# Layer norm statistics in five groups, key constants of two groups set by GpSimd, and a store wait split in two

## The reference

```
q, k, v = y @ Wq.T + bq, y @ Wk.T + bk, y @ Wv.T + bv      # y = layernorm(x), 16 heads of 8
attn    = softmax(q k^T / sqrt(8)) * head_mask
x       = x + (attn v) @ Wo.T + bo
z       = layernorm(x)
x       = x + shared_ffn(z) + sum over the top 2 of 8 experts of gate_e * ffn_e(z)
```

## Time and profile before

| | |
|---|---|
| median of 3 runs | 617.31 us |
| the profiled execution | 620.32 us |
| its span | 618.5 us |
| PE busy | 601.8 us, 97% |
| DVE busy | 494.4 us, 80% |
| ACT busy | 445.3 us, 72% |
| POOL busy | 281.0 us, 45% |
| granted TensorE clock | 0.999 of full speed |

### The profile page before, as it was taken

One profiled execution on the slowest core, in us unless ns is written; L12 is line 12 of the kernel. 1 busy time (PEld: TensorE's weight loads), 2 busy tenths in 40 slices (PEclk: granted clock), 3 DMA queues, 4 the chain that ended last, 5 costly groups with the idle time before them and its releaser, 6 DMA issues. The chain is left out here.

```text
span 618.5 us, 21763 instructions
## 1 busy us (share of the span) xinstructions
PE 601.8 (97%) x8263; PEld 389.9 (63%) x8263; DVE 494.4 (80%) x1077; ACT 445.3 (72%) x967; POOL 281.0 (45%) x481
## 2 busy tenths in 40 slices
PE   7999999999999999999999999999999999999998
PEld 3544555555445545545545545447899999989966
DVE  8899999998988988988988988536366666666557
ACT  5878988888888888887887887973455555555551
POOL 7946711422641642542542542566454445545510
PEclk9999999999999999999999999999999999999999
DMA  6887343342443131131131230003222222212174
GB/s 174 246 279 210 86 98 89 111 113 79 122 123 88 55 95 47 54 97 51 50 96 50 51 97 12 17 31 78 53 66 65 64 68 60 68 56 66 47 263 153
DMA packets 43983, 57.66 MB, mean 93 GB/s; under 512 B 11146, under 2 KB 31754, under 8 KB 43898
## 3 DMA queue, kind: packets, MB, share of 16 engines
q1 hardware_dynamic: 39578, 47.59, 27.3%
q0 software_dynamic: 4320, 8.89, 4.4%
HBM read 35.76 MB, written 20.42 MB: 91 GB/s over the span
## 5 line engine op out<-in xcount | busy, mean ns | idle before, releaser
L1020 DVE TENSOR_REDUCE mx<-ps 128x2 f32<-128x1024 f32 x256 | 304.1, 1211 | 28.1 <-PE ps L1460 23.7
L883 ACT ACTIVATE probs<-ps 128x512 f32<-128x512 f32 x512 | 290.0, 601 | 46.4 <-PE ps L1488 32.7
L1488 PE MATMUL ps<-q_op,k_op 128*32 128x512 bf16 x2048 | 199.9, 380 | 2.2 <-ACT probs L883 1.2
L1460 PE MATMUL ps<-k_op,q_op 96*32 96x512 bf16 x2048 | 158.2, 380 | 2.6 <-DVE mx L1020 2.0
L1503 PE MATMUL ps<-probs,v_op 128*32 128x256 f32 x2048 | 157.6, 378 | 0.2 <-ACT probs L883 0.2
L941 ACT ACTIVATE probs<-ps,b_cur 128x128 f32<-128x128 f32 x284 | 80.9, 368 | 67.2 <-PE ps L1704 54.1
L759 POOL DMA_INDIRECT results<-rest,row_id x71 | 73.0, 1028 | 77.1 <-DVE rest L1330 60.0
L1488 PEld LDWEIGHTS ps<-q_op,k_op 128*32 128x32 bf16 x2048 | 58.6, 95 | 59.4 <-ACT probs L883 11.9
L650 POOL DMA_INDIRECT slots<-route_sb,slot_u x64 | 63.6, 993 | 68.8 <-ACT probs L883 59.5
L1460 PEld LDWEIGHTS ps<-k_op,q_op 96*32 96x32 bf16 x2048 | 55.1, 96 | 61.4 <-DVE mx L1020 22.1
L1503 PEld LDWEIGHTS ps<-probs,v_op 128*32 128x32 f32 x2048 | 65.3, 109 | 41.6 <-issue 0.9
(11 more groups left out here) (180 smaller groups left out, 554.2 us busy)
## 6 DMA issues: line engine op xcount, KB each, us to landing
q_op<-q_scr SPq DMA_DIRECT2D x96, 96.0 KB
k_op<-k_scr SPq DMA_DIRECT2D x96, 96.0 KB
w_sb<-in_W SPq DMA_DIRECT2D x18, 256.0 KB
probs<-slots SPq DMA_DIRECT2D x71, 64.5 KB
q_scr<-w_sb SPq DMA_DIRECT2D x8, 384.0 KB, 3.7
k_scr<-w_sb SPq DMA_DIRECT2D x8, 384.0 KB, 3.9
k_scr<-w_sb SPq DMA_DIRECT2D x8, 256.0 KB, 4.4
probs<-results SPq DMA_DIRECT2D x4, 512.0 KB, 4.8
```

The costliest lines, as they stand in the source:

```text
L883: nc.scalar.activation(probs[:, i, j, :], ps[:, BANK["key", b, hg, s], :], ACT.Exp, scale=float(D) ** -0.5).then_inc(s_exp, 1)
L1020: nc.vector.reduce_max(mx[:, slot % 2, 2 * p:2 * p + 2], ps[:, bank:bank + 2, :], AX.X).then_inc(s_max, 1)
L1460: last = nc.tensor.matmul(ps[c, BK_A + a % 4, :], q_op[hg][0:SH, j, P * i + c.start:P * i + c.stop], k_op[hg][0:SH, j, :], start=True, sto ...
L1488: last = nc.tensor.matmul(ps[c, bank, :], k_op[hg][:, j, P * i + c.start:P * i + c.stop], q_op[hg][:, j, :], start=True, stop=True)
```

## The change

The statistics of sequences 4 to 7 become two groups: {4, 5}, made where the group of four was, and {6, 7}, made by VectorE in sequence 2, with their power and product on GpSimd after the third parts of sequence 2. The minus ones of head groups 2 and 3 are set by GpSimd, over all 128 rows of `k_op`, and the zeros are written over rows 0 to 95 afterwards; for group 3 all of this moves from sequence 1 to sequence 3. The stores of sequence 0 get semaphores of their own, one for q and one for k, and the first group's loads are issued q first, three of q after the q store has landed, then three of k after the two k stores have. `wait_stored` gives all other users of the store semaphores the same waits as before, with the counts of `s_scr[0]` lower by one round. Blank lines are left out:

```diff
         s_w1st, s_wom = sem("first_weights_loaded"), sem("wo_masked")
+        s_q0, s_k0 = sem("first_q_parts_stored"), sem("first_k_parts_stored")
...
+        def wait_stored(eng, b):
+
+            if b == 0:
+                eng.wait_ge(s_q0, 16)
+                eng.wait_ge(s_k0, 16 * (N_SCR - 1))
+            elif b > 0:
+                eng.wait_ge(s_scr[b % DEEP], (b // DEEP + (b % DEEP > 0)) * (16 * N_SCR))
+
...
-        LN1_SEQS = ((0,), (1,), (2, 3), (4, 5, 6, 7))
+        LN1_SEQS = ((0,), (1,), (2, 3), (4, 5), (6, 7))
         POOL_SEQ = 3
         LN1_TILES = [slice(NT * some[0], NT * (some[-1] + 1)) for some in LN1_SEQS]
         LN1_OF = [n for n, some in enumerate(LN1_SEQS) for _ in some]
...
                 sp.wait_ge(s_lo, 2 * b + 1)
-                sp.dma_start(to_q, parts[u][:, 0, :, :]).then_inc(s_scr[u], 16)
+                sp.dma_start(to_q, parts[u][:, 0, :, :]).then_inc(s_scr[u] if b else s_q0, 16)
                 sp.wait_ge(s_mid, 2 * b + 2)
                 sp.wait_ge(s_lo, 2 * b + 2)
-                sp.dma_start(to_k[:, 0:PARTS, :], parts[u][:, 1, :, :]).then_inc(s_scr[u], 16)
-                sp.dma_start(to_k[:, PARTS:K_PARTS, :], parts[u][:, 1, 0:K_PARTS - PARTS, :]).then_inc(s_scr[u], 16)
+                sp.dma_start(to_k[:, 0:PARTS, :], parts[u][:, 1, :, :]).then_inc(s_scr[u] if b else s_k0, 16)
+                sp.dma_start(to_k[:, PARTS:K_PARTS, :], parts[u][:, 1, 0:K_PARTS - PARTS, :]).then_inc(s_scr[u] if b else s_k0, 16)
             def load_group(b, hg):
                 wait(sp, s_sb, (b * HG + hg - HG + 1) * (J * NT))
                 if b == 0:
                     sp.wait_ge(s_zero[hg], N_ZERO)
-                if hg == 0:
-                    sp.wait_ge(s_scr[b % DEEP], (b // DEEP + 1) * (16 * N_SCR))
-                for r in range(PARTS):
-                    for scr, op, first in ((q_scr, q_op, 0), (k_scr, k_op, D * r)):
-                        src = scr[b, :, :].rearrange("(x h) t -> x h t", h=H)[first:first + PR, J * hg:J * (hg + 1), :]
-                        sp.dma_start(op[hg][PR * r:PR * (r + 1), :, :], src).then_inc(s_ld[hg], 16)
+                if hg == 0 and b > 0:
+                    wait_stored(sp, b)
+                uses = [(r, w) for r in range(PARTS) for w in range(2)]
+                if (b, hg) == (0, 0):
+                    uses.sort(key=lambda use: use[1])
+                for r, w in uses:
+                    if (b, hg, r) == (0, 0, 0):
+                        sp.wait_ge((s_q0, s_k0)[w], 16 * (1, N_SCR - 1)[w])
+                    scr, op, first = ((q_scr, q_op, 0), (k_scr, k_op, D * r))[w]
+                    src = scr[b, :, :].rearrange("(x h) t -> x h t", h=H)[first:first + PR, J * hg:J * (hg + 1), :]
+                    sp.dma_start(op[hg][PR * r:PR * (r + 1), :, :], src).then_inc(s_ld[hg], 16)
...
                 if e == 0:
                     for u in range(DEEP):
-                        sp.wait_ge(s_scr[u], (B // DEEP) * (16 * N_SCR))
+                        wait_stored(sp, B - DEEP + u)
...
             def zero_scores(hg):
                 nc.gpsimd.memset(q_op[hg][:, :, :].bitcast(f32), 0.0).then_inc(s_zero[hg], 1)
+                if hg >= 2:
+                    nc.gpsimd.memset(k_op[hg][:, :, :].bitcast(f32), TWO_MINUS_ONES).then_inc(s_zero[hg], 1)
+                    pool.wait_ge(s_zero[hg], 2)
                 nc.gpsimd.memset(k_op[hg][0:SH, :, :].bitcast(f32), 0.0).then_inc(s_zero[hg], 1)
...
                 if b == 0:
                     normalise(POOL_SEQ)
                     ln1_rstd(3)
-                elif b == 1:
+                elif b == 3:
                     zero_scores(3)
                 elif b == 2:
+                    ln1_rstd(4)
                     nc.gpsimd.memset(v_op[:, :, :, :, :], 0.0).then_inc(s_pad, 1)
                     pool.wait_ge(s_pad, 2)
                     for hg in range(HG):
...
                 ready, bias, bank = ((s_qp, bq_sb, q_bank(b)), (s_kp, bk_sb, k_bank(b)))[w]
                 act.wait_ge(ready, b + 1)
-                wait(act, s_scr[b % DEEP], b // DEEP * (16 * N_SCR))
+                wait_stored(act, b - DEEP)
                 nc.scalar.activation(parts[b % DEEP][:, w, 0, :], ps[:, bank, :], ACT.Identity, bias=bias[:, 0:1]).then_inc(s_hi, 1)
...
             def ln1_stats(n):
                 some = LN1_TILES[n]
-                dve.wait_ge(s_x[n], 16)
+                dve.wait_ge(s_x[min(n, 3)], 16)
                 for t in range(some.start, some.stop):
                     last = nc.vector.bn_stats(stats[:, t, :], x_sb[:, t, :])
                 last.then_inc(s_st, 1)
...
                 if b == 0:
                     ln1_stats(3)
                     ln1_moments(3)
-                if b in (1, 2):
-                    set_key_ones(1 + b)
+                if b == 2:
+                    ln1_stats(4)
+                    ln1_moments(4)
                 first_max(b, 2)
```

## The result

The changed kernel is slower: median 619.39 us (616.75 to 621.18, 20 runs) against 617.63 us (616.6 to 619.02, 20 runs), a ratio of 1.0024 with a 95% interval of 1.0015 to 1.0033. I had forecast 616.1 us, from the 617.31 us of the first three runs. The single executions fall in two clusters. Six of the 20 have a mean granted clock of 0.999 or 1.0 and a median of 617.18 us; fourteen have 0.997 or 0.994 and a median of 619.91.

The account below looks back on a forecast made before the run. TensorE's long stretch bounds the kernel, its start set by ScalarE's chain in the projection stage. A gain of 1.22 us, other edits adding nothing, gave 617.31 - 1.22 = 616.1 us; range 615.3 to 617.7.

Parts of the forecast that it names:

- The path through the group of 16: Projection stage: eight tiles instead of 16 free VectorE 1.61 us earlier; ScalarE's k part of sequence 2 comes 1.22 earlier.
- The sets moved off VectorE: Two constant sets, 2.36 us with issue, leave VectorE for GpSimd; little worth alone, but make room for the moved tiles.
- the earlier loads: On SP, q loads go before k loads, the last issued 1.1 us earlier; worth 0 alone, protecting up to 1.1.
- the moved half: Eight tiles of statistics moved into sequence 2 on VectorE take 2.40 us; cost 0.0, at most 0.1, or 0.2 uncovered.
- The cover: VectorE's idle 1.01 us before 29.13, taken to cover its 0.2 us lag behind ScalarE at the remainder of sequence 3.
- Rival 3: GpSimd's constant sets, at about 30.5 to 33.4, hold VectorE by up to 2.85 us: 618.9 us; chance 0.08.
- Rival 1: The k loads land late, delaying row scores to 24.3; 0.3 to 0.6 gain left, 616.7 to 617.0 us; chance 0.12.
- Rival 2: The TensorE-bound stretch sets its own start, so earlier inputs only wait and nothing is gained: 617.3 us; chance 0.12.
- the power of sequences 2 and 3: On GpSimd, behind the added constant set, its issue was forecast 0.15 us later; cost 0, at most 0.1.

Follow-up runs that it names:

- r2: Changed kernel with GpSimd taking the fifth group's power before the third parts in sequence 2; 598.52 us, ratio 0.9985 to the kernel before.
- r8: The kernel before the change, unchanged, profiled again on another chip; 600.09 us in one run.
- r6: Kernel of r2 with the minus ones of head groups 2 and 3 set by VectorE again; 602.26 us, ratio 1.0045 to the kernel before.
- r5: Kernel of r2 without the split store wait, loads of the first group as before the change; 598.73 us, ratio 0.9989 to the kernel before.
- r4: Changed kernel with statistics in four groups again, keeping GpSimd's constants and the split wait; 599.41 us, ratio 0.9999 to the kernel before.
- r9: Changed kernel with GpSimd's third parts of sequence 2 replaced by constant sets that read nothing; 619.41 us, ratio 0.9980 to the kernel before.
- r1: The changed kernel as it is, run again on another chip; 601.09 us, ratio 1.0024 to the kernel before.
- r3: Changed kernel with six more unused matmuls on TensorE after the row scores of sequence 3; 599.52 us, ratio 1.0001 to the kernel before.
- r10: Kernel of r2 with none of the five keeping matmuls before the first transposes; 619.16 us, ratio 0.9973 to the kernel before.

## Why the prediction was wrong

**Right: where the gain comes from and how large it is.** The path through the group of 16, ScalarE's idle time and TensorE's k projection, 1.22 us with 0.39 of 1.61 lost, stands, though VectorE came 1.27 us earlier and not 1.61: it was TensorE's k projection that set ScalarE's k part, at 18.89 on the old scale as forecast. r2 shows the gain, 38.30 to 37.08 (and 38.35 in r8, its wait of 0.38 taken off). The whole kernel gained 0.9 of it. The sets moved off VectorE are what lets it through (r6), and the earlier loads spare TensorE an idle time of 1.51 (r5's profile); by themselves both are worth nothing (r4).

**The step that failed: the moved half.** "Cost of the moved half: 0.0, at most 0.1; if the cover were gone, 0.2." I took the length of the group, 2.40 us, from a place where GpSimd, beside the seven steps, only set constants or stood idle, and moved it beside the third parts of sequence 2. There it takes 4.01 us from the start of its tiles to the start of its last step (21.54 to 25.55), and r9 shows the cause: without the reads of the third parts the same three steps take 0.17 at most. The remainder of sequence 3 came 1.55 us later than forecast, not 0.0 to 0.2. I had checked for each engine when its operand would be there, and not what the two do to each other while both are busy. The cover that I had named, 1.01 us before 29.13, was on the wrong side: TensorE's q projection of sequence 4 asks for the remainder itself, since it writes over its bank, and does so 1.2 us earlier than in the kernel before (24.4 against 25.6).

**The term that was not there: the clock.** VectorE's lateness alone brings the gain to zero (r1's profile, r3). That the kernel is slower comes from TensorE's fall to 1.2 GHz behind the idle times of 1.47 and 0.60 us, in 14 of 20 and 5 of 9 executions. It costs 2.7 us between the medians of the clusters in the first set of runs and 2.0 in r1. The profiled stages differ by 1.63 (39.93 and 38.30); where the rest goes is not shown.

**Rival 3 was nearly it, with the wrong pair.** I asked whether GpSimd's constants hold VectorE's long instructions, and gave it 0.08, arguing from statistics that ran beside them unhindered. As asked it is refuted: beside the three sets of 31.93 to 34.78 in the changed kernel a remainder takes 0.75 and a maximum 1.22, as before. The evidence of the statistics was good for `bn_stats`, which has one input, and I let it stand for steps with two. The same trace had small steps beside reading instructions of GpSimd, the power at 6.00 to 6.51 and the normalising at 16.67 to 17.28, and they took 0.15 to 0.20 us there; beside third parts it had none, so it could not show the price; I should have bounded it by the length of GpSimd's instruction, 1.16 us for each that meets one, and the rival would have been worth more.

**Rival 1** (late k loads) did not happen in the changed kernel, whose row scores came at the forecast date. It was undervalued as the condition: without the split wait TensorE idles 1.51 (r5), where I gave the edit 0 to 1.1 and had the landing as at most 3 us after the issue. From the issue to TensorE's start it took 4.0, with the stores of sequence 1 behind it on the same queue.

**Rival 2** fell with r2: the stretch bound by TensorE does start earlier. **What was wrongly costed at nothing but did no harm**: the set of 10.09 holds the moment step at 10.13 by 0.77 us, and the power of sequences 2 and 3 on GpSimd was late by 0.5, where I had 0.15, and nobody waited for it.

## What to carry to other kernels

When a step moves, list what runs beside it in the new place on the engine with which it shares a port, and read off how many of its operands each side takes from SBUF; its length from the old place holds only if the neighbours are alike, and rows beside another reader do not settle it: here the third parts held the steps, and the power and the normalising hardly did. Idle time on TensorE is to be priced by what the clock may do after it too, and not by its own length alone: look at the spread of the mean clock over executions, not only at one profile. And when a step is moved to free a chain, try the other engine's order as well: here one line on GpSimd turned 0.24% slower into 0.15% faster.

## What was not expected of the hardware

Seven steps of eight elements per partition, 0.17 us each alone, can cost 1.6 us more together, when two of them start while GpSimd makes a third part. A single `tensor_scalar` of eight elements took 0.93 us beside a constant being set. In 19 of 29 executions of the changed kernel the mean clock is 0.997 or 0.994. The profiled one of them shows a fall to half behind idle times of 1.47 and 0.60 us; the profiled one of the other ten shows the same idle times (1.48 and 0.60) and no fall. With 1.70 and 0.60 it fell in 5 of 5 (r6), with the first filled and 0.60 left in 0 of 11 (r3), with 1.51 alone in 0 of 11 (r5); the idle times are those of the one profile of each. So one idle time of this length had no fall behind it in these runs, and two close together had one in most. What decides it in a single execution stays open. The start of the useful work differed by 0.93 us between two executions of one program (8.07 and 9.00), with the lengths of the matmuls ahead of it. With no keeping matmuls it started at 8.02 (r10), and with all five once too (r9).
